# Edge-maximum passes of a graph network: gathered rows in two half-precision parts, list loads, and 13 instead of 11 blocks by products

## The reference, cut to what matters

```
m   = relu(x @ Wp + bp)                                  # 3125 x 96
agg = segment_max(m[src], dst, num_segments=3125)        # over 50,000 edges
out = x @ Ws + agg @ Wn + b
```

## Time and profile before

| what | us |
|---|---|
| timed runs, median of three | 2963.22 (2958.58 to 2969.26) |
| the profiled execution's own time | 2943.83 |
| its span, first to last instruction | 2942.1 |
| busy: PE, DVE, ACT, POOL | 2528.8, 1978.5, 1227.1, 1216.1 |
| max1: first gather to the issue of the last | 719.6 to 1243.8 |
| max2: first gather to the issue of the last | 1350.5 to 1871.5 |
| propagation, from 2130 us to the end | 812 |

### The profile page before, as it was taken

How to read it: one execution, slowest core, us unless ns; L and a number is a source line. 1 busy time by engine, 2 the same in 40 slices (tenths; PEclk the granted TensorE clock), 3 DMA queues, 4 the chain that set the end, 5 groups by cost and what they waited for, 6 DMA issues and landing times. The chain is left out here.

```text
span 2942.1 us, 67814 instructions
## 1 busy us (share of the span) xinstructions
PE 2528.8 (86%) x26419; PEld 1892.6 (64%) x26419; DVE 1978.5 (67%) x6078; ACT 1227.1 (42%) x2920; POOL 1216.1 (41%) x1429
## 2 busy tenths in 40 slices
PE   6998999996778888747888888458799999999999
PEld 3444777773445544434455545337699999999999
DVE  7997999996788988726888888441244444444444
ACT  5997888884334444423444334330221111111110
POOL 2001999993677777634777777411000000000000
PEclk8998999997899998857999989659999999999999
DMA  6002000004343434342343444509700000000000
GB/s 197 1 1 91 12 13 12 12 12 112 93 111 107 121 109 114 104 88 68 108 120 108 112 112 137 160 8 321 239 2 2 2 2 2 2 2 2 2 2 18
DMA packets 163890, 208.87 MB, mean 71 GB/s; under 512 B 82829, under 2 KB 129194, under 8 KB 162896
## 3 DMA queue, kind: packets, MB, share of 16 engines
q1 hardware_dynamic: 135772, 165.27, 19.0%
q0 software_dynamic: 24256, 37.90, 5.3%
q10 hardware_dynamic: 3540, 1.30, 0.2%
HBM read 104.70 MB, written 102.05 MB: 70 GB/s over the span
## 5 line engine op out<-in xcount | busy, mean ns | idle before, releaser
L1782 POOL DMA_INDIRECT max_row<-table,max_src_rows x696 | 768.5, 1104 | 367.6 <-issue 240.4
L2349 PE MATMUL prop<-g,adj 128*128 128x192 f16 x9216 | 770.9, 246 | 7.1 <-PEq L2020 7.1
L2349 PEld LDWEIGHTS prop<-g,adj 128*128 128x128 f16 x9216 | 759.8, 98 | 14.9 <-issue 12.4
L1677 POOL TENSOR_SCALAR e<-e 128x512 f32<-128x512 f32 (+1 forms) x625 | 366.9, 606 | 244.4 <-ACT e L1665 228.0
L1691 DVE TENSOR_TENSOR e<-e,a_ps 128x1024 f32<-128x1024 f32 (+1 forms) x313 | 371.6, 1194 | 38.6 <-PE a_ps L1603 16.6
L2438 ACT ACTIVATE g<-prop_state 128x96 f16<-128x96 f32 (+1 forms) x375 | 106.0, 283 | 635.3 <-DVE prop_state L2406 635.3
L1665 ACT ACTIVATE e<-s_ps 128x512 f32<-128x512 f32 (+1 forms) x625 | 335.7, 585 | 62.3 <-PE o_ps L1615 38.8
L1822 PE MATMUL max_strip_ps<-max_key_hot,max_lane_w 128*128 128x400 f16 x1200 | 296.2, 361 | 72.4 <-issue 36.2
L2404 DVE SCALAR_TENSOR_TENSOR part<-prop,coef,prop_base 128x96 f32<-128x96 f32 x384 | 120.6, 314 | 312.9 <-PE prop L2349 225.5
L1875 DVE TENSOR_SCALAR max_lane_w<-iota,max_tables 128x128 f16<-128x128 f16 x1200 | 319.6, 313 | 0.0
L1812 PE MATMUL max_far<-adj 128*96 128x512 f16 x1100 | 285.9, 398 | 11.8 <-issue 11.6
(11 more groups left out here) (263 smaller groups left out, 3382.3 us busy)
## 6 DMA issues: line engine op xcount, KB each, us to landing
weights<-max_rows_w SPq DMA_DIRECT2D x52, 400.0 KB
rows_dram<-max_out SPq DMA_DIRECT2D x100, 192.0 KB
weights<-adj SPq DMA_DIRECT2D x48, 400.0 KB
ws_w<-weights SPq DMA_DIRECT2D x50, 384.0 KB, 5.2
rows_dram<-adj SPq DMA_DIRECT2D x96, 192.0 KB
ws_w<-weights SPq DMA_DIRECT2D x50, 288.0 KB, 4.5
max_row<-table,max_src_rows POOLq DMA_INDIRECT x696
ws_w<-weights SPq DMA_DIRECT2D x50, 128.0 KB, 2.8
```

The costliest lines, as they stand in the source:

```text
L1677: nc.gpsimd.tensor_scalar(e_tile(u), e_tile(u), math.exp(10.0), math.exp(-10.0), ALU.min, ALU.max).then_inc(clipped, 1)
L1782: nc.gpsimd.indirect_dma_start(row[i % RING][:, j, :], None, table_dram, bass.IndirectOffsetOnAxis(ap=src_rows[:, 4 * n + j:4 * n + j + 1] ...
L2349: return nc.tensor.matmul(sums(step, t), adj[:, k, t * P:(t + 1) * P], states[:, k, :], start=start and t % 2 == 0, stop=k == END - 1 and ...
```

## The change

- `FAR` becomes `range(6, 92, 7)`: 13 blocks go by products, and 85 are gathered instead of 87. Two PSUM banks (`far_ps[j % 2]`, the second is the one that `same_ps` had) let the far tiles run in every step: `first` is one step earlier.
- The table in DRAM holds the two float16 parts of `m`, side by side, in the same 384 bytes a row. The two layers before the passes store it from the parts, after `lo_kept`, and no longer from `out`. `turn_rows` becomes eight float16 products with the identity instead of four float32 transposes.
- `spread_same` and `keep_same` go. SP loads each block's `same`, 1 KB spread over 96 partitions, from DRAM: four before the loop, then one a block behind the row store.
- `low_part` moves from DVE to ACT. PE first adds minus the high part to the PSUM bank (`take_high`, a product with `minus`, the identity times -1) and ACT copies what is left.
- In `walk_adjacency`, which runs only when a list overflows, 625 unrolled products become a loop.

```diff
-FAR = range(7, 88, 8)
+FAR = range(6, 92, 7)
@@ first_layer (second_layer alike)
-                sp.wait_ge(pooled, t + m)
-                sp.dma_start(node_view(table)[:, t:t + m, :], out[:, g % 2, 0:m, 0, :]).then_inc(stored[g % 2], 16)
                 sp.wait_ge(own_kept, t + m)
                 sp.dma_start(node_view(self_dram)[:, t:t + m, :], out[:, g % 2, 0:m, 1, :]).then_inc(stored[g % 2], 16)
+                sp.wait_ge(lo_kept, g + 1)
+                sp.dma_start(node_view(table)[:, t:t + m, :], parts[:, t:t + m, :, :].rearrange("p t a d -> p t (a d)").bitcast(F32)).then_inc(table_stored, 16)
@@ max_pass
-                first, last = FAR[j - 1] + LEAD + 1 if j >= 1 else 1, n + LEAD - 1
+                first, last = FAR[j - 1] + LEAD if j >= 1 else 1, n + LEAD - 1
@@ tensor
-            def spread_same(n):
...
                 for j in range(4):
-                    tr = nc.tensor.transpose(col_ps[i % 2][0:D, j * P:(j + 1) * P], row[i % RING][:, j, :], c.ident[:, :])
-                tr.then_inc(turned, 1)
+                    for a in range(2):
+                        mm = nc.tensor.matmul(col_ps[i % 2][0:D, j * P:(j + 1) * P], row_parts[i % RING][:, j, a, :], c.ident16[:, :],
+                                              start=a == 0, stop=a == 1, skip_group_check=True)
+                mm.then_inc(turned, 1)
...
-                if k == 0 and j >= 1:
-                    pe.wait_ge(scanned, FAR[j - 1] + 1)
+                if k == 0 and j >= 2:
+                    pe.wait_ge(scanned, FAR[j - 2] + 1)
...
+            def take_high(n):
+                pe.wait_ge(hi_kept, n + 1)
+                nc.tensor.matmul(strip_ps[n % 2][:, 0:KEYS], minus[:, :], strip_at(0, n).rearrange("p k d -> p d k"),
+                                 start=False, stop=True, skip_group_check=True).then_inc(hi_taken, 1)
...
                 for j, k in far_tiles(m):
                     add_far(j, k)
+                if m < PARTS:
+                    take_high(m)
@@ vector
-            def low_part(n):
-                dve.wait_ge(hi_kept, n + 1)
-                nc.vector.tensor_tensor(strip_at(1, n), strip_ps[n % 2][:, 0:KEYS].rearrange("p (d k) -> p k d", d=GROUP),
-                                        strip_at(0, n), ALU.subtract).then_inc(lo_kept, 1)
@@ scalar
-            def keep_same(n):
...
+            def low_part(n):
+                act.wait_ge(hi_taken, n + 1)
+                nc.scalar.activation(strip_at(1, n), strip_ps[n % 2][:, 0:KEYS].rearrange("p (d k) -> p k d", d=GROUP), ACT.Copy).then_inc(lo_kept, 1)
@@ sync
+            def load_same(n):
+                if n >= SAME:
+                    sp.wait_ge(scanned, n - SAME + 1)
+                at = n * BLK
+                sp.dma_start(same[n % SAME][:, :], same_dram[at:at + BLK].rearrange("(a e) -> a e", a=1).to_broadcast([D, BLK])).then_inc(same_loaded[n % SAME], 16)
...
+                    if n + SAME < NB:
+                        load_same(n + SAME)
```

More of the change, by code:

```diff
@@ L148, in load_joint_weights, with first_layer @@
     queue.dma_start(w[D:D + 1, D:2 * D], row(second_bias)).then_inc(loaded, 16)
-def first_layer(nc, c, res_dram, xh_dram, x_dram, Wp, bp, Ws, b, table, parts, self_dram, numbers, lists):
+def first_layer(nc, c, res_dram, xh_dram, x_dram, Wp, bp, Ws, b, table, parts, self_dram, numbers, minus, lists):
     RINGS, OUTS = 4, 5
@@ L1720, in max_pass @@
         row = [sb(f"row{i}", [P, 4, D], F32) for i in range(RING)]
+        row_parts = [r[:, :, :].rearrange("p j d -> p (j d)").bitcast(F16).rearrange("p (j a d) -> p j a d", j=4, a=2) for r in row]
         same = [sb(f"same{i}", [D, BLK], F16) for i in range(SAME)]
@@ L1726, in max_pass @@
         col_ps = [ps(f"col{i}") for i in range(2)]
-        back_ps, far_ps = ps("back"), ps("far")
-        same_ps = ps("same_ps")
+        back_ps, far_ps = ps("back"), [ps(f"far{i}") for i in range(2)]
         gathered = [c.gather_sem(f"{name}_gathered{i}") for i in range(RING)]
@@ L1731, in max_pass @@
         rows_stored = [sem(f"rows_stored{i}") for i in range(2)]
-        turned, cleared, scanned, spread, same_kept, back, kept, zero_out = (
-            sem("turned"), sem("cleared"), sem("scanned"), sem("spread"), sem("same_kept"),
-            sem("back"), sem("kept"), sem("zero_out"))
+        same_loaded = [sem(f"same_loaded{i}") for i in range(SAME)]
+        turned, cleared, scanned, back, kept, zero_out = (
+            sem("turned"), sem("cleared"), sem("scanned"), sem("back"), sem("kept"), sem("zero_out"))
         key_hot = sb("key_hot", [P, WIN, KEYS], F16)
@@ L1843, in turn_back @@
                 tr.then_inc(back, 1)
-            for n in range(SAME - 1):
-                spread_same(n)
             for m in range(NB + LEAD):
@@ L1919, in _ @@
                     far_hot(j, k)
-                if m < PARTS:
-                    low_part(m)
         @block.scalar
         def _(act):
-            def keep_same(n):
-                act.wait_ge(spread, n + 1)
-                if n >= SAME:
-                    act.wait_ge(scanned, n - SAME + 1)
-                nc.scalar.activation(same[n % SAME][:, :], same_ps[0:D, :], ACT.Copy).then_inc(same_kept, 1)
             def high_part(n):
@@ L1959, in _ @@
                     high_part(m)
-                if n >= 0 and n + SAME - 1 < NB:
-                    keep_same(n + SAME - 1)
+                if m < PARTS:
+                    low_part(m)
                 if m >= PARTS:
```

83 lines of the change are left out of this document (42 added, 41 removed).

## The result

Kernels in turns on one chip, device time in us:

| | median | lowest, highest | runs |
|---|---|---|---|
| before | 2967.49 | 2958.36, 2976.05 | 13 |
| changed | 2976.59 | 2965.24, 2990.60 | 13 |

The account below looks back on a forecast made before the run. GpSimd's gathers were taken to set the pace: 340 x 1.255 + 60.4 + 23 = 510 us a pass against 524.2 and 521.0. With the layers +1 that is -24 us, 2939 us; range 2915 to 2955.

Parts of the forecast that it names:

- Bubbles: GpSimd's waits for a free buffer in each pass: from 34 us down to 23, bounds 7 and 45.
- if waits for buffers grow past 40 us: Sign that the forecast falls: GpSimd's waits for buffers above 40 us, where near 23 us was expected.
- Gathers: GpSimd in each pass: two gathered blocks fewer, 8 gathers at 1.255 us, 10.0 us less.
- Tiles, priced by steps: Gathers held up beside one-hot tiles: 0.65 us per step with tiles, 93 steps for 80, 8.6 us more a pass.
- This buys nothing directly: Low part leaving VectorE: 29 us less VectorE work per seven blocks, no direct gain as GpSimd is the limit; bounds 0 to 34.
- take_high: TensorE's new product in each step, 400 columns read with a stride: 0.17 to 0.42 us.
- ACT even: ScalarE's work: -95 x 0.589 us for the lists, +100 x 0.505 for the low parts, about even and hidden.
- lists hidden: Loading each block's list by DMA from SP: hidden, 0 to 5 us, DMA share up by 0.07.
- layers +1 us: Layers before the passes, table stored from the parts: last store 0 to 1 us later per layer, 0.5 taken.
- B: Rival: a trade, one 2.5 us bubble in each of 13 rounds, 0 to +4 us a pass, 2960 to 2970; 0.15 with D.
- D: Rival: no effect on the passes' pace, GpSimd's gain and loss cancelling, 2955 to 2972 us; counted with B, 0.15 together.
- rival C: TensorE takes over the pace at take_high through an uncovered round with ScalarE, slower: 2987 to 3035 us; chance 0.2.

Follow-up runs that it names:

- e9: The changed kernel run again, in a set where the kernel before takes 2943 us: ratio 1.0047 to the kernel before.
- e5: The kernel before, unchanged, profiled again in a set without late hand-overs: one run, 2831.31 us.
- e6: The changed kernel, unaltered, run in a set without late hand-overs: ratio 0.9942 to the kernel before.
- e1: The changed kernel with take_high reading without a stride and writing PSUM with one, 13 blocks by products: ratio 0.9922 to the kernel before.
- e7: The changed kernel with take_high reading without a stride and 11 blocks by products instead of 13: ratio 0.9887 to the kernel before.
- e2: The changed kernel with the low part back on VectorE and no take_high, 13 blocks by products: ratio 1.0039 to the kernel before.
- e8: The changed kernel with the low part back on VectorE, no take_high and 11 blocks by products; lists and parts remain: ratio 0.9988 to the kernel before.
- e12: The changed kernel with take_high read without stride, 11 blocks by products, and every one-hot tile written twice: one run, 3015.59 us.
- e16: Repeat of e1 (changed kernel, take_high read without stride, 13 blocks by products) in another set: ratio 0.9911 to the kernel before.
- e13: Repeat of e7 (changed kernel, take_high read without stride, 11 blocks by products) in another set: ratio 0.9885 to the kernel before.
- e3: The changed kernel with 11 blocks by products instead of 13, all else kept: ratio 0.9954 to the kernel before.
- e10: The changed kernel with take_high read without stride and 5 blocks by products instead of 13: ratio 1.0262 to the kernel before.
- e11: The changed kernel with take_high read without stride and 2 blocks by products instead of 13: ratio 1.0312 to the kernel before.
- e18: e10 (5 blocks by products, take_high read without stride) plus a one-column GpSimd memset after each block's four gathers: ratio 0.9908 to the kernel before.

## Why the prediction was wrong, step by step

**Failed: "Bubbles. ... I keep half of the middle (10), the start (10), and 3 for seven last blocks: 23 us."** They were 45 and 53 us, and 52 and 50 in e9. The two passes took 1067 us where the sum had 1020: of these 47 us the bubbles are 52, the held-up gathers -8, the rest 3. I had read that bubbles come where a step without tiles comes, from eight blocks without one. That is not borne out: the changed kernel has tiles in every step from 1 to 93 and more waits than before. What the runs show in its place is that the waits come with late hand-overs, which a whole set has or hasn't. In a set that has them, 43 of the changed kernel's 47 late ones come after five or more gathers without a pause; in the others there are none, and the kernel is faster. The prediction named this size as what would make it fall ("if waits for buffers grow past 40 us").

Where no hand-over is late the forecast of 0.8% looks nearly right: from e5 to e6 the passes changed by -8.8 and -6.2 us, and the whole by -0.58%. As to the change, that is luck. Without bubbles the prediction's sums for a pass, 436.7 + 51.8 = 488.5 us before and 426.7 + 60.4 = 487.1 after, lie within 4 us of what e5 and e6 took, but they give a gain of 1.4 us a pass, and the 0.8% came from bubbles that were to go. Two terms were wrong, in opposite ways:

- **Gathers**: -10.0 us a pass; right. With 1.255 us a gather and the held-up time, each pass without waits adds up to within 2 us.
- **Tiles, priced by steps, +8.6**: too little. By tiles it is +13.4 and +15.5 (e1 against e7), 14 (e2 against e8), and e12 gives 0.25 to 0.27 us a tile; e16 against e13 gives 20 and 12, e6 against e3 11 and 7. The Trainium skill (SBUF, State Buffer, section Who interferes with whom) has VectorE's two-port instructions and GpSimd exclude each other for the whole instruction, for which the prediction had worked out 14 us and not taken it. The first three comparisons agree with the page; the last two scatter around it. They don't say it for every instruction: from 5 blocks to 2 (75 tiles) only 7 to 9 us go.
- **"This buys nothing directly"**, of the low part leaving VectorE: wrong. It buys 15 us a pass of held-up gathers (e2 against e1; 14 and 16 by e8 against e7). By these prices the sum where nothing waits is -10 + 15 - 15 = -10 us a pass, and 9 and 6 were measured.
- **take_high**, at most 0.42 us: 0.83 by its record. The cause is the strided read: without it 0.51 (46.7 us for 92 in e7). The kernel gains 0.7% by that with 11 blocks (e3 against e7), and 0.2 to 0.3% with 13 (0.9922 and 0.9911 against 0.9942; these intervals overlap).
- **ACT even, lists hidden, layers +1 us**: right. ScalarE is busy 1220.3 us against 1227.1; e8 has the ratio 0.9988; the DMA share went up by 0.08, as against 0.07 worked out.

**The rivals.** In time (2976.59 us) the result falls between B and D, up to 2972, and C, from 2987. By its signs **rival C** came nearest: waits near 50 us and TensorE standing before `take_high`. But its mechanism, a round of TensorE and ScalarE that is uncovered in each step, isn't it: in e6 the same round costs 3.6 us a pass. What it may do is pass lateness on. In the kernel before, nothing of TensorE's step waited for ScalarE's copy of the same step; now `take_high` does, and everything behind it. In e9, as in the first trace of the changed kernel, TensorE stands before it:

```profile
L1834 PE MATMUL max_strip_ps<-max_strip,minus_ident 128*128 128x400 f16 x95 | 79.0, 832 | 68.5 <-issue 48.6 <-ACT max_strip L1933 19.7
```

That this is what made the waits grow from 34 to 45 us and more is argued, not shown. The other candidates are that the low part no longer holds gathers up, and `take_high`'s strided read. The kernels that tell them apart are e2 and e1 in a set with late hand-overs, and both fell in others (e10 and e11, which read without a stride, wait even more, but have fewer tiles). Open as well is what makes hand-overs late at times.

## What to carry to other kernels

An engine that sets the pace can be held up by another's instructions: price an edit by what it takes from and gives to that hold (here some 0.27 us a tile, and 0.15 us a low part behind tiles), and not by the idle time of the engine that runs it. An unexplained wait in the profile is the weakest term of a sum: here its growth, of 10 to 20 us a pass, decided the sign, so neither half of it nor none should be booked as gain. And a change of half a per cent may have one sign in one set of runs and the other in the next, perhaps on the same chip; look whether the wait that it lives on is there.

## What the runs showed of the hardware

- In two of seven sets of runs (the comparison above and e9 to e12), ScalarE takes up many of TensorE's results some 2 to 5 us late, mostly after GpSimd has issued five or more gathers without a pause; in the five others it never does (0 of 97, 98 and 95 copies in e5, e6 and e18, and none in the other traces of these sets that hold all gathers). The kernel before takes 2967 and 2943 us in the two, 2834 to 2839 in the five, at nearly the same clock (0.92 and 0.93). From its first trace to e5, 31 to 32 us lie in each pass, 28 between the passes (106.7 us against 78.7), and 22 behind them (1070.6 against 1049.0).
- A gather beside a run of one-hot tiles lasts beyond the last of them: in e7 the 156 that overlap three or four tiles take 1.4 and 1.8 us on average, and end 0.1 to 0.2 us after the last tile (117 of them) or 0.8 to 0.9 us after it (33). One that overlaps no tile takes 0.95 to 0.97 us, with or without a low part beside it (e2).
- A float16 product over 400 columns takes 0.83 us if its moving operand is read with a stride of 256 bytes (e6), 0.51 us if neighbours are read and the output has the stride (e7).
- A memset of one column on GpSimd is 0.15 us long on average (0.12 at the median), and the gather behind it starts 0.19 us after its end (e18).
